# Rows of 128 edges issued one by one from SyncE and ScalarE in the weighted stages and in the sort of a graph kernel

## What is computed

```python
h = relu(norm(x)); x = x + segment_sum(h[src] * weight, dst) @ W.T + b          # weighted
h = relu(norm(x)); x = x + mlp(sum, max, mean of edge_attr (32 wide) by src)    # pooled
h = relu(norm(x)); x = x + relu(.2 h + .8 * sum of (h @ Wr[type])[src] / deg)   # relation
h = relu(norm(x)); x = x + elu(softmax-weighted sum of h[src] over dst)         # attention
```

## Time and profile before

| | |
|---|---|
| median of 3 runs | 16737.31 us (16735.06 to 16739.51) |
| profiled execution | 16717.65 us, of which the span is 16715.9 |
| GpSimd busy | 12576.4 us, 75% of the span |
| VectorE busy | 8380.9 us, 50% |
| ScalarE busy | 2611.6 us, 16% |
| TensorE busy | 2071.2 us, 12% |
| DMA | 1141.43 MB, mean 68 GB/s |

### The profile page before, as it was taken

The page is one execution under the profiler, slowest core; times in us unless marked ns, Lnnn a source line. Parts: engine busy times, 40 slices in busy tenths (PEclk is TensorE's granted clock), DMA queues, the critical chain, the costliest instruction groups (busy, mean ns, idle before and its releaser), DMA issues. The chain is left out here.

```text
span 16715.9 us, 114264 instructions
## 1 busy us (share of the span) xinstructions
PE 2071.2 (12%) x17217; PEld 1933.7 (12%) x17217; DVE 8380.9 (50%) x5953; ACT 2611.6 (16%) x1261; POOL 12576.4 (75%) x13194
## 2 busy tenths in 40 slices
PE   1212333333333111101320000000000000000000
PEld 1212333333323100101210000000000000000000
DVE  7878988888888677777621111111131222222222
ACT  0000111110101232232221111111110110111101
POOL 7777777777777777777767777777777777777776
PEclk9998666666666555555565555555555555555555
DMA  4222211112121233333532222222233222222222
GB/s 80 55 53 68 71 64 63 68 61 70 61 70 61 89 112 114 108 114 108 103 101 56 56 51 56 56 56 51 56 54 41 57 57 52 57 57 57 52 57 56
DMA packets 686784, 1141.43 MB, mean 68 GB/s; under 512 B 407713, under 2 KB 459500, under 8 KB 644044
## 3 DMA queue, kind: packets, MB, share of 16 engines
q0 software_dynamic: 421952, 380.03, 12.4%
q1 hardware_dynamic: 209740, 325.53, 6.6%
q10 hardware_dynamic: 54336, 428.56, 6.4%
HBM read 613.30 MB, written 519.84 MB: 68 GB/s over the span
## 5 line engine op out<-in xcount | busy, mean ns | idle before, releaser
L1079 POOL DMA_INDIRECT by_src<-H,sort_place_i x3224 | 3122.1, 968 | 983.7 <-issue 983.1
L559 POOL DMA_INDIRECT rel_G<-rel_table,rel_idx x3118 | 2945.7, 945 | 984.6 <-issue 951.3
L559 POOL DMA_INDIRECT att_G<-att_table,att_idx x3118 | 2942.2, 944 | 951.3 <-issue 951.3
L559 POOL DMA_INDIRECT lead_rows<-h_table,wsum_idx x3044 | 2887.2, 948 | 927.7 <-issue 927.7
L753 DVE SCALAR_TENSOR_TENSOR rel_Gf<-rel_Sf,rel_keep_first,rel_Gf 128x64 f32<-128x64 f32 x55 | 18.7, 341 | 3386.3 <-ACT rel_Gf L884 3386.3
L727 DVE TENSOR_TENSOR_SCAN att_near<-att_near,er_in 128x60 f32<-128x60 f32 (+2 forms) x55 | 19.3, 351 | 2835.1 <-issue 1846.7
L1247 PE MATMUL pG<-sort_cnt,sort_lowT 128*128 128x98 f32 x6448 | 1116.0, 348 | 816.7 <-DVE sort_prod L1137 816.7
L1247 PEld LDWEIGHTS pG<-sort_cnt,sort_lowT 128*128 128x128 f32 x6448 | 1071.6, 261 | 824.9 <-DVE sort_prod L1137 824.9
L951 PE MATMUL wsum_C<-wsum_high,wsum_low 128*128 128x98 fp8e4 x6448 | 560.9, 282 | 3369.2 <-DVE wsum_high L604 3369.2
L951 PEld LDWEIGHTS wsum_C<-wsum_high,wsum_low 128*128 128x128 fp8e4 x6448 | 520.1, 142 | 3410.6 <-issue 3410.6
L603 DVE TENSOR_TENSOR wsum_low<-iota_b,wsum_parts 128x3840 fp8e4<-128x3840 bf16 x216 | 891.7, 4128 | 9.8 <-DVE wsum_parts L594 9.8
(11 more groups left out here) (368 smaller groups left out, 7624.2 us busy)
## 6 DMA issues: line engine op xcount, KB each, us to landing
rel_G<-rel_table SPq DMA_DIRECT2D x8480, 0.2 KB
att_G<-att_table SPq DMA_DIRECT2D x8480, 0.3 KB
scan_att<-att_S ACTq DMA_DIRECT2D x53, 1980.0 KB
scan_wsum<-wsum_S ACTq DMA_DIRECT2D x53, 1920.0 KB, 6.5
sort_keys<-key_rows SPq DMA_DIRECT2D x53, 1920.0 KB, 9.6
scan_rel<-rel_S ACTq DMA_DIRECT2D x53, 1920.0 KB
scan_pool<-pool_S ACTq DMA_DIRECT2D x70, 1440.0 KB
rel_G<-rel_table ACTq DMA_DIRECT2D x5088, 0.2 KB
```

The costliest lines, as they stand in the source:

```text
L559: pool.indirect_dma_start(out=G[s][:, j, :], out_offset=None, in_=table, in_offset=bass.IndirectOffsetOnAxis(ap=idx[s][:, j:j + 1], axis=0 ...
L1079: pool.indirect_dma_start(out=by_src, out_offset=bass.IndirectOffsetOnAxis(ap=place_i[s][:, j:j + 1], axis=0), in_=row[s][:, j, :], in_off ...
```

## The change

In the weighted stages the last two columns of chunks 1 to 52 are no longer gathered by GpSimd but row by row, 160 by SyncE and 96 by ScalarE, as in the relation stage. In the sort the last two columns of each full chunk are scattered row by row, 144 by SyncE and 112 by ScalarE. The places of these rows, in bytes, are written to DRAM and read back into one partition (two DMAs of SyncE) behind the loads of the next chunk. ScalarE issues its part for chunk k-1 within chunk k, between its first and its second counter copy. In the pooled stage the loads of the sorted rows move from SyncE to ScalarE, and ScalarE issues its 96 rows before it takes the pooled result out. In the first third ScalarE waits for the ids and issues its rows of chunk 1 ahead of the square root; both engines issue the rows of chunks 18 and 19 (gathered ahead) before that block ends.

```diff
-    COLUMNS = dict(wsum=0, sort=0, rel=2, att=2)
-    BY_SP = dict(wsum=0, rel=160, att=160)
+    COLUMNS = dict(wsum=2, sort=2, rel=2, att=2)
+    BY_SP = dict(wsum=160, sort=144, rel=160, att=160)
...
@@ weighted stages, SyncE
-                        for k in range(1, c1 + 1):
+                        for k in range(1, c1 + 2):
                             rows_of_chunk(k)
                         sp.wait_ge(rows_stored, 96)
                     if pooled:
...
-                        load_rows(0, 0, SIDE)
-                        for k in range(1, NC):
-                            rows_of_chunk(c0 + k + 1)
-                            load_rows(k // 2, k % 2, SHORT if k == NC - 1 else SIDE)
+                        for k in range(2, NC):
+                            rows_of_chunk(c0 + k)
@@ weighted stages, ScalarE
                     if raw:
+                        single.await_moved(act)
+                        act_rows_of_chunk(1)
                         act.wait_ge(raw_var_ready, 1)
                         nc.scalar.activation(raw_root[:], raw_var[:], ACT.Sqrt).then_inc(raw_root_ready, 1)
...
+                    def load_rows(k, w=SIDE):
+
+                        act.wait_ge(pscanned, k + 1)
+                        act.dma_start(prow[:, 0:w, :], sorted_rows(0)[:, k * SIDE:k * SIDE + w, :]).then_inc(prow_loaded, 16)
+                        act.dma_start(prow[:, w:w + 1, :], sorted_rows(1)[:, k * SIDE + w - 1:k * SIDE + w, :]).then_inc(prow_loaded, 16)
...
                         act.wait_ge(pscanned, k + 2)
+                        if k + 1 < NC:
+                            load_rows(k + 1, SHORT if k + 1 == NC - 1 else SIDE)
                         for half in range(2):
...
                         own(i, s)
+                        act_rows_of_chunk(c0 + 2 * i + s + 2)
                         if pooled:
                             take_pooled(2 * i + s)
-                        act_rows_of_chunk(c0 + 2 * i + s + 2)
...
+                    if pooled:
+                        await_scattered()
+                        load_rows(0)
...
                     own(NC // 2 - 1, 1, FINAL, False)
+                    if counts and not pooled:
+                        act_rows_of_chunk(c1 + 1)
@@ sort, SyncE and ScalarE
+                def issue_rows(engine, k, s, rows, landed):
+
+                    wide = 4 * (A + 1)
+                    of = row[s].rearrange("p j f -> p (j f)").bitcast(U8)
+                    to = by_src.rearrange("n f -> (n f)").unsqueeze(0).bitcast(U8)
+                    for r0 in range(rows.start, rows.stop, BATCH):
+                        registers = [engine.alloc_register(f"sort_row{k}_{r}") for r in range(r0, r0 + BATCH)]
+                        engine.load(registers, place_row[s][:, r0:r0 + BATCH])
+                        for r, register in enumerate(registers, r0):
+                            n, p = r // P, r % P
+                            at = (L - SC + n) * wide
+                            place = engine.snap(register, donate=True, min_val=0, max_val=wide * (EP + 1))
+                            engine.dma_start(to[:, bass.ds(place, wide)], of[p:p + 1, at:at + wide]).then_inc(landed[k % TURNS], 16)
...
                         sp.wait_ge(place_ready, k + 2)
                         sp.wait_ge(rows_ready, k + 3)
+                        sp.dma_start(single_places[s].rearrange("(n p) -> p n", p=P), place_bytes[s], allow_slow_non_contiguous=True).then_inc(places_moved, 16)
                         sp.wait_ge(places_moved, 32 * k + 16)
+                        sp.dma_start(place_row[s], single_places[s].unsqueeze(0)).then_inc(places_moved, 16)
                         sp.wait_ge(places_moved, 32 * k + 32)
+                        issue_rows(sp, k, s, sort_by_sp, scattered_sp_rows)
 
                     for k in range(NCH - 1):
                         load_chunk(k, k % 2)
-                        if k == 0 and lead_single:
-                            lead_single.issue(sp, lead_chunk, range(0, P), lead["rows"][1][:], h_table, lead["sp_rows"])
-                        if k and COLUMNS["sort"]:
+                        if k:
                             scatter_rows(k - 1, (k - 1) % 2)
...
                         for g in range(len(ways)):
                             snapshot(k * STEPS + g, s * STEPS + g)
+                            if g == 0 and k and sort_by_act:
+                                act.wait_ge(places_moved, 32 * k)
+                                act.wait_ge(rows_ready, k + 2)
+                                issue_rows(act, k - 1, 1 - s, sort_by_act, scattered_act_rows)
                             if g in fills:
                                 fill_rows(k, i, s, fills[g], w)
```

More of the change, by code:

```diff
@@ L196, in build @@
                     gathered=[semaphore(f"lead_gathered{s}") for s in range(2)],
[L197 to L198 removed]
+                    sp_rows=[semaphore(f"lead_sp_rows{q}") for q in range(TURNS)],
+                    act_rows=[semaphore(f"lead_act_rows{q}") for q in range(TURNS)])
+        sort_by_sp, sort_by_act = range(0, BY_SP["sort"]), range(BY_SP["sort"], COLUMNS["sort"] * P)
+        scattered_sp_rows = [semaphore(f"scattered_sp_rows{q}") for q in range(TURNS)]
+        scattered_act_rows = [semaphore(f"scattered_act_rows{q}") for q in range(TURNS)] if sort_by_act else []
         scattered = [semaphore(f"scattered{s}") for s in range(2)]
@@ L412, in gathered_layer @@
                 sp_rows = lead["sp_rows"] if counts else [sem(f"sp_rows{q}") for q in range(TURNS)] if by_sp else []
-                act_rows = [sem(f"act_rows{q}") for q in range(TURNS)] if by_act else []
+                act_rows = lead["act_rows"] if counts else [sem(f"act_rows{q}") for q in range(TURNS)] if by_act else []
                 def await_rows(engine, i, s, w=L):
@@ L839, in _, with act_rows_of_chunk, await_scattered @@
                         nc.scalar.copy(idx[s][:], index[:, (c0 + s) * L:(c0 + s + 1) * L]).then_inc(index_ready, 1)
+                    def act_rows_of_chunk(k):
+                        if by_act and k < FULL:
+                            act.wait_ge(turned, k - c0 + 1)
+                            single.issue(act, k, by_act, G[k % 2][:], table, act_rows)
                     if raw:
+                        single.await_moved(act)
+                        act_rows_of_chunk(1)
                         act.wait_ge(raw_var_ready, 1)
                         nc.scalar.activation(raw_root[:], raw_var[:], ACT.Sqrt).then_inc(raw_root_ready, 1)
+                    def await_scattered():
+                        act.wait_ge(scattered[0], 16 * (L - COLUMNS["sort"]) * (NCH // 2))
+                        act.wait_ge(scattered[1], 16 * (L - COLUMNS["sort"]) * (NCH // 2 - 1) + 16 * LAST)
+                        for q in range(TURNS):
+                            chunks = len(range(q, FULL, TURNS))
+                            act.wait_ge(scattered_sp_rows[q], 16 * len(sort_by_sp) * chunks)
+                            if sort_by_act:
+                                act.wait_ge(scattered_act_rows[q], 16 * len(sort_by_act) * chunks)
+                    def load_rows(k, w=SIDE):
+                        act.wait_ge(pscanned, k + 1)
+                        act.dma_start(prow[:, 0:w, :], sorted_rows(0)[:, k * SIDE:k * SIDE + w, :]).then_inc(prow_loaded, 16)
+                        act.dma_start(prow[:, w:w + 1, :], sorted_rows(1)[:, k * SIDE + w - 1:k * SIDE + w, :]).then_inc(prow_loaded, 16)
                     def turn_pooled(k, w=SIDE):
@@ L907, in own_and_pooled @@
                         own(i, s)
+                        act_rows_of_chunk(c0 + 2 * i + s + 2)
                         if pooled:
                             take_pooled(2 * i + s)
-                        act_rows_of_chunk(c0 + 2 * i + s + 2)
-                    for k in range(2):
-                        act_rows_of_chunk(c0 + k)
+                    if not counts:
+                        for k in range(2):
+                            act_rows_of_chunk(k)
+                    if pooled:
+                        await_scattered()
+                        load_rows(0)
                     for i in range(0, NC // 2 - 1):
@@ L1150, in hand_on @@
                         dve.wait_ge(rows_used, k + 2)
-                        if COLUMNS["sort"] and n == L:
-                            v.tensor_scalar(place_bytes[s][:], place[s][:, L - 1:L], rank[:, L - 1:L], float(4 * (A + 1)), ALU.add, ALU.mult)
+                        if n == L:
+                            for m in range(SC):
+                                j = L - SC + m
+                                v.tensor_scalar(place_bytes[s][:, m:m + 1], place[s][:, j:j + 1], rank[:, j:j + 1], float(4 * (A + 1)), ALU.add, ALU.mult)
                         v.tensor_tensor(place_i[s][:, 0:n], place[s][:, 0:n], rank[:, 0:n], ALU.add).then_inc(place_ready, 1)
```

49 lines of the change are left out of this document (12 added, 37 removed).

## The result

The changed kernel takes 17501.12 us in the median of 4 runs (17486.72 to 17505.0), against 16736.62 us before: a ratio of 1.0455, with a 95% interval of 1.0437 to 1.0473. The forecast was 17447 in 16,860 to 17,700. The profiled execution has a span of 17503.3 us, 787.4 more than before.

What follows compares the result with a forecast made beforehand. GpSimd, never waiting, was taken as the bound. Sort +715.7 us less 6 in the pooled stage made +710 on the profiled 16717.65; with 19.7 for the median, 17447 us, range 16,860 to 17,700.

Steps and rivals of the forecast that it cites:

- The loop in the sort: Sort: loads, moves of places, ScalarE's rows and counters follow one another, 89.5 us a round against GpSimd's 73.8.
- Step a: Sort: SyncE's loads of the next chunk hold up the moves of the places until 11.6 us behind the places.
- Step b: Sort: two moves of the places in sequence, 5.2 us with their issue (4.8 to 8).
- Step c: Sort: ScalarE issues 112 rows at 0.459 us each, 51.4 us (bounds 45 to 56).
- d, counters 2 to 6 and the picks: Sort: from ScalarE's second counter copy to the next places, 21.3 us.
- rival A: Sort round of 89.5 us (84 to 93.5), pooled stage by 60 either way: 17,150 to 17,720 us; chance 0.65.
- Rival B: Sort: the loads don't hold up the places; round of 79 us, +153, so 16,890 us; chance 0.20.
- Rival C: Sort: the loop fits under GpSimd's 73.8 us, so GpSimd never waits; -123, 16,615 us; chance 0.08.
- R: Any round of the sort's loop; the change adds 53 x R - 4034 us and breaks even at 76.1.
- SyncE second: Sort: SyncE's own round of loads, moves and rows is 80 us, over GpSimd's 73.8 but only second.
- Start and end of the first third: First weighted stage: GpSimd waits some 41 us for chunk 0; block ends at 1475, 24 us late; first scatter 1550.6.
- The pooled stage: Pooled weighted stage: ScalarE's round of 74.0 us sets the pace, tail 19 us longer; about 6 us gained.

Runs made afterwards that it cites:

- the places turned: Changed kernel with the places turned into a row by TensorE and VectorE instead of two DMAs: 16647.41 us, 0.9959 of the kernel before.
- The other queue: Changed kernel with ScalarE, not SyncE, issuing the two moves of the places in the sort: 17353.76 us.
- the run with 160 and 96 rows: Changed kernel with 160 rows by SyncE and 96 by ScalarE in the sort, instead of 144 and 112: 17333.35 us.
- the last kernel: Changed kernel with places turned on TensorE, first third mended, one column by SyncE alone in chunks 18 to 53: 16538.07 us, 0.9893 of the kernel before.
- the sort's part alone: Changed kernel without single rows in the weighted stages: 26311.57 us, on a chip where the kernel before takes 24130.15.

## Why the prediction was right

**What bounds the kernel.** GpSimd without waits, 1.273 and 1.249 us a column: right. With the places turned, 106 columns gave 132.9 of 135 us.

**The loop in the sort**, the step that carried the sum: right in kind and, by luck, in size. 89.5 us forecast, 89.9 measured in the mean. Its parts in the round shown:

| step | forecast | measured |
|---|---|---|
| a, the loads | 11.6 | 11.7 (3804.1 to 3815.8) |
| b, the two moves | 5.2 | 9.2: 7.0 behind the loads' end, then 2.2 to the register load at 3825.0 |
| c, 112 rows with their loads | 51.4 | 47.5 |
| d, counters 2 to 6 and the picks | 21.3 | 20.6 |

Step b failed in size. I took the gather's 2.4 us for each move and let 4.8 to 8 stand as bounds; with nothing in front, the first alone took 8.2, over the upper bound for both. The nearest row was a bad one: a gather moves 128 pieces of 256 bytes, this move 256 pieces of 4. Step c was too dear by 3.9. Some 2.3 of them are the first register load: I had read 96 rows with the 3.1 us that it takes behind a large store (9023.97 to 9027.09 in the earlier trace rows), and in the sort, where no store of ScalarE stands in front, it takes 1.3. The other 1.5 are the rows, 0.413 us each (46.22 over 112) against 0.426 (40.93 over 96). The errors in b and c cancel.

**Step a and the queue.** That the moves wait for the loads was right on SyncE's queue: the first one ends 7.0 us behind the end of the loads, and alone it takes 8.2. By the Trainium skill, DMA: Bandwidth & Descriptors, section Queues, rings and completion order, each DMA engine takes a queue's descriptors in the order of its ring; the trace agrees, with the 7.0 us behind the loads' end. But I had made 10 us a round of it, the whole distance between A and B. The other queue gave back 2.8 only, because there both moves ran beside the loads and took 12.1 and some 5 us in the mean; and with the places first, the 8.2 stayed. Rival B (79) was thus near, though not as it stood: without the loads in front, a round is 81.2 and the time 17044.79, because of step b, not 16,890.

**Rival C** (under 73.8, and faster) decided at R = 76.1. The pieces of 8 bytes bring R to 75.0 and the kernel to 16705.64, the turn on TensorE to GpSimd's pace and 16647. At 75.0 the sum gives 59 us gained, and 11 were measured, so the break-even lies near 75.2: the sum had the pooled stage 44 us too cheap. The mechanism was right; what I had not seen is that the moves, not the rows, were the part that could go.

**SyncE second**, at 80: right, 79.5 in the round shown, and by the run with 160 and 96 rows.

**Start and end of the first third.** Chunk 0 free at 207: 207.5 (200.89 + 6.61). GpSimd's wait: 36.8, not 41, since it came to it later, at 171.5 and not 165.4: two of its gathers of chunk 1 took 4.3 and 3.9 us. Such gathers were there before the change as well (the maximum of 4321 ns in the earlier trace rows), and I had counted all at the median. The block's end: 1475 forecast, 1476.1 measured, and the first scatter 1552.1 against 1550.6. I wrote "some 24" for the wait that would be seen there; what shows is 34.7. The 24 were the block's lateness against the kernel before; by my own numbers GpSimd was through with chunk 18 at 1440, 35 us before 1475.

**The pooled stage** is where the rest of the error lies. ScalarE's round was the right bound, but 74.0 was too short by 1.3 us. The wait for the first half's store is 1.5 longer, 6.9 instead of 5.4, and I had taken the 5.4 over from a kernel in which SyncE loaded the sorted rows. ScalarE now loads them just ahead of that store. That this is what lengthens the wait isn't shown: it is 5.3 us in the mean of 36 before, 6.8 after, and 6.0 in the last kernel, where ScalarE still loads them but issues no single rows. 32 rounds of 1.3 make 42 us. The tail of +19 was right (20.2). In rival A's range the pooled stage was added at the upper end only; with 60 us off, the lower end is 17,095, not 17,150.

**The sum.** Of the 77.4 us between +710 and +787.4: 22 in the sort (0.4 us a round), 44 in the pooled stage with its tail, 1.5 at the start, and 9.6 in stages that the change doesn't touch. The last I can't explain; in the kernel with the turned places the relation stage, for one, took 3897.9 us against 3896.0 before and 3901.7 after. The forecast of 17447 is nearer to the median, by 54 us, than the spans are: I had added 19.7 for the median over the profiled execution, and this time the median was 3.9 below it. That part is luck.

## What to carry to other kernels

Work taken from a bound engine is free only if its replacement fits into the round of whoever does it. List that engine's program order, look for a wait that closes a loop through it (here: places, moves, rows, counters, places), and add the loop up before counting the saving. When a loop is over, look first at its dead parts: the two moves of 1 KB took 12 to 21 us a round, the batch of rows that was shifted to and fro 6.6, and a small matrix product did the work of the moves in 2.

## What the runs showed of the hardware that was not expected

**Small pieces.** A move of 1 KB out of 128 partitions to DRAM: 8.2 us in 256 pieces of 4 bytes, 2.6 us in 128 pieces of 8, with the DMA engines some 7% busy in both. Beside 3,840 KB of loads on another queue the first form takes 12.1 us in the mean, and the loads are held up by it as well: 31 GB/s for 2 us, and an end 9 us later in the chunk shown. A read of one 1 KB piece beside the loads then takes some 5 us in the mean and 7 in the chunk shown, against 2.3 (120.3 us in 53 waits) in the changed kernel, where nothing large is under way.

**The issue of single rows was half as fast on one chip.** Where the kernel before takes 24130.15 us instead of 16716, ScalarE's 112 rows of a chunk took this (timeline of the sort's part alone, then the line's ns min/median/max):

```profile
6100.31 94.06 ACTq L1047 DMA_DIRECT2D by_src<-H  x112
...
L1047 ACTq DMA_DIRECT2D by_src<-H x5936: 3/230/1410, 1867.8 to 9073.6; - x198
```

and on the other chip, in the changed kernel, 46.2 us with

```profile
L1046 ACTq DMA_DIRECT2D by_src<-H x5936: 230/230/545, 1575.3 to 6296.7; - x198
```

The median of an issue is the same, 230 ns, but single ones last up to 1.4 us, and 112 rows take twice as long; GpSimd's indirect DMAs are as before there (0.946 us in the mean). All four of the changed kernels that ran there were as slow, 26312 to 28619 us. Whether it is the chip or something that passes, and by what, was not tried. GpSimd waits in the relation stage too, which the change doesn't touch:

```profile
POOL rel_G L547 <- ACT rel_idx L882: 2699.4, 51, 72.6
```

The attention stage has a wait like it, 2778.4 us. I read both as the single rows that these stages already have. Moving more columns off GpSimd costs more than it saves there: the sort's part added 2181 us to the kernel before.
